# First offset convolution ahead of the second pair's sums, a new order of small sums and roundings, and the first result stored by halves

## The reference

```python
# block 1: a bottleneck with a modulated deformable 3x3 convolution
out = relu(group_norm(conv1x1(x, w1), gn1))            # 256 -> 64 channels, 32 groups
om = conv3x3(out, w_off) + b_off                       # 27 rows: 9 x offsets, 9 y offsets, 9 masks
sampled = bilinear_sample(out, py, px) * sigmoid(mask) # 9 taps
out = relu(group_norm(einsum(sampled, w2), gn2))
x = relu(group_norm(conv1x1(out, w3), gn3) + x)        # 64 -> 256 channels

# block 2: the same shape, weights rounded to powers of two, activations to 16 bits
h = conv1x1(quant(x), w1q)
h = relu(bn1(depthwise3x3(quant(h), pegq) + peg_b))
h = relu(bn2(conv3x3(quant(h), w2q)))
x = relu(bn3(conv1x1(quant(h), w3q)) + x)
# quant(t): scale = max(|t|)/32767; round(t/scale)*scale, one scale for the whole tensor
```

## Time and profile before

| what | us |
|---|---|
| runs | 90.78, 89.81, 90.74 |
| median | 90.74 |
| the profiled execution | 90.92 |
| its span, first to last instruction | 89.1 |

### The profile page before, as it was taken

The page is one execution under the profiler, slowest core; times in us unless marked ns, Lnnn a source line. Parts: engine busy times, 40 slices in busy tenths (PEclk is TensorE's granted clock), DMA queues, the critical chain, the costliest instruction groups (busy, mean ns, idle before and its releaser), DMA issues.

```text
span 89.1 us, 2173 instructions
## 1 busy us (share of the span) xinstructions
PE 74.9 (84%) x893; PEld 51.4 (58%) x893; DVE 64.8 (73%) x174; ACT 49.6 (56%) x88; POOL 5.0 (6%) x10
## 2 busy tenths in 40 slices
PE   5986999996899898999999999899579877779600
PEld 1332666474698797889988896355223374555400
DVE  0224539999999789999896725899895784867850
ACT  4203165679974999996868003807562254632660
POOL 7601010000000000000003100000000000000000
PEclk9999999999999999999999999999999999999999
DMA  1999800000000000000000000000000000000076
GB/s 29 328 318 324 329 9 0 0 7 0 0 7 0 0 0 7 4 11 0 0 7 0 0 0 7 0 0 0 0 0 0 0 0 0 0 7 4 0 256 215
DMA packets 3274, 4.17 MB, mean 47 GB/s; under 512 B 256, under 2 KB 2688, under 8 KB 3264
## 3 DMA queue, kind: packets, MB, share of 16 engines
q1 hardware_dynamic: 2992, 3.76, 12.7%
q10 hardware_dynamic: 272, 0.26, 0.9%
HBM read 2.98 MB, written 1.05 MB: 45 GB/s over the span
## 4 chain that ended last, share of the span: by engine, by line
PE 43%; DVE 29%; ACT 12%; DMA 6%; issue 4%; SPq 2%; DVEq 0%; ACTq 0%
PE acc L488 15%; PE slot L475 9%; DVE g_rows L912 9%; DMA x_sb<-x 6%; PE acc L616 4%; DVE g_cols L1014 3%; ACT g_cols L813 3%; PE acc L595 3%; PE slot L403 3%; ACT g_cols L720 2%; PE slot L524 2%; DVE g_cols L1055 2%; ACT pad L777 2%; PE slot L556 2%; DVE unused L1031 2%
## 5 line engine op out<-in xcount | busy, mean ns | idle before, releaser
L912 DVE TENSOR_TENSOR g_rows<-hats 128x2304 f32<-128x2304 f32 (+1 forms) x12 | 20.6, 1752 | 0.1
L720 ACT ACTIVATE g_cols<-slot 128x768 f32<-128x768 f32 x24 | 17.8, 830 | 3.7 <-PE slot L475 3.7
L488 PE MATMUL acc<-g_cols,v_sb 128*64 128x128 f32 x288 | 17.7, 276 | 0.0
L488 PEld LDWEIGHTS acc<-g_cols,v_sb 128*64 128x64 f32 x288 | 15.5, 137 | 1.1 <-issue 0.3
L366 PE MATMUL slot<-zeros 128*128 128x512 bf16 x54 | 14.8, 409 | 1.0 <-DVE zeros L832 1.0
L475 PE MATMUL slot<-consts_sb,g_rows 64*128 64x64 f32 x288 | 11.8, 226 | 2.1 <-DVE g_rows L912 1.7
L475 PEld LDWEIGHTS slot<-consts_sb,g_rows 64*128 64x128 f32 x288 | 10.3, 140 | 3.9 <-DVE g_rows L912 2.7
L366 PEld LDWEIGHTS slot<-zeros 128*128 128x128 bf16 x54 | 5.5, 109 | 6.9 <-issue 2.1
L777 ACT ACTIVATE pad<-g_cols 64x256 bf16<-64x256 int8 x8 | 3.3, 418 | 4.9 <-DVE g_cols L1055 4.8
L843 DVE BATCH_NORM_STATS2 stats<-acc 128x6 f32<-128x256 f32 x4 | 1.7, 431 | 4.3 <-PE acc L378 2.6
L403 PE MATMUL slot<-feat,woff_sb 128*64 128x256 f32 x36 | 4.7, 385 | 0.0
(11 more groups left out here) (137 smaller groups left out, 116.4 us busy)
## 6 DMA issues: line engine op xcount, KB each, us to landing
out<-g_cols SPq DMA_DIRECT2D x4, 256.0 KB, 2.3
x_sb<-x SPq DMA_DIRECT2D x3, 256.0 KB, 4.7
wq_sb<-wq SPq DMA_DIRECT2D x1, 484.5 KB, 6.5
woff_sb<-woff SPq DMA_DIRECT2D x1, 288.0 KB, 5.7
w_sb<-w SPq DMA_DIRECT2D x1, 288.0 KB, 5.8
x_sb<-x ACTq DMA_DIRECT2D x1, 256.0 KB, 3.1
w_sb<-w SPq DMA_DIRECT2D x1, 256.0 KB, 6.5
consts_sb<-consts SPq DMA_DIRECT2D x1, 232.0 KB, 5.7
```

The costliest lines, as they stand in the source:

```text
L488: mm = nc.tensor.matmul(acc[b2][rows(h), at:at + P], v_sb[:, B2 * h + b2, q, k, :], g_cols[t][h][:, NQ * k + q, :], start=(k == 0 and q == ...
L720: nc.scalar.activation(dst.rearrange("p k (r n) -> p k r n", r=HALVES), src.rearrange("p r (k n) -> p k r n", k=per), ACT.Copy).then_inc(g ...
L912: tt(g_rows[i % 3][:, taps], hats[:, t, h, 1, taps].unsqueeze(3).to_broadcast(shape), hats[:, t, h, 0, taps].unsqueeze(2).to_broadcast(sha ...
```

## The change

It has four parts.

1. PE's opening. The three idle matmuls before `pair_sums(2, 1)` go. Steps 0 and 1 of the offset convolution of pair 0 are issued ahead of `pair_sums(2, 1)`, steps 2 to 4 behind it; then comes `make_v(0)`, and only then the offset convolution of pair 1.
2. In the group norm over eight, for pair 1, the means matmul goes from ahead of the deviations matmul to behind `eight_vars`, with a semaphore `mean_done` of its own, which DVE now waits for.
3. The first rounding of block 2. DVE makes the quotients of (b2, c) = (0,0), (0,1 in image pair 1: written `quot[:, 0, 1]`) and `quot[:, 1, 1]`, and takes `ROUND` from `quot[:, 0, 0]` and `quot[:, 1, 1]`. ACT makes the quotient of `quot[:, 1, 0]` itself, and takes `ROUND` from it and from `quot[:, 0, 1]`. The indices of `quot` are c, then b2.
4. The first of four result pieces is handled and stored in two halves, one image each, so `PIECES` has five entries.

```diff
-PIECES = ((0, 0, 0, 2), (1, 0, 0, 2), (0, 1, 0, 2), (1, 1, 0, 2))
+PIECES = ((0, 0, 0, 1), (0, 0, 1, 1), (1, 0, 0, 2), (0, 1, 0, 2), (1, 1, 0, 2))
...
             conv1(1)
-            idle(IDLE[2], spare)
-            pair_sums(2, 1)
...
-            pe.wait_ge(woff_in, 16)
-            for b2 in range(B2):
-                pe.wait_ge(feat_ready, b2 + 1)
-                for s in range(TAPS_A):
-                    mm = om_step(b2, s)
-                    if b2 == 1 and s == 1:
-                        pe.wait_ge(consts_in, 16)
-                        om_turn(0)
-                mm.then_inc(om_done, 1)
...
-            for i in range(4):
+            pe.wait_ge(woff_in, 16)
+            pe.wait_ge(feat_ready, 1)
+            for s in range(TAPS_A):
+                mm = om_step(0, s)
+                if s == 1:
+                    pair_sums(2, 1)
+            mm.then_inc(om_done, 1)
+            pe.wait_ge(w2_in, 16)
+            make_v(0)
+            pe.wait_ge(feat_ready, 2)
+            for s in range(TAPS_A):
+                mm = om_step(1, s)
+                if s == 1:
+                    pe.wait_ge(consts_in, 16)
+                    om_turn(0)
+            mm.then_inc(om_done, 1)
+            for i in range(1, 4):
                 make_v(i)
...
-                nc.tensor.matmul(small[b2][:, 8:12], avg8, mv[:, b2, :, 0], start=True, stop=True)
+                if b2 == 0:
+                    nc.tensor.matmul(small[b2][:, 8:12], avg8, mv[:, b2, :, 0], start=True, stop=True)
...
+                if b2 == 1:
+                    nc.tensor.matmul(small[b2][:, 8:12], avg8, mv[:, b2, :, 0], start=True, stop=True
+                                     ).then_inc(mean_done, 1)
...
-                    if (b2, c) == LAST_WHOLE:
-                        pe.wait_ge(whole_by_dve, 1)
+                    if b2 == c:
+                        pe.wait_ge(whole_by_dve, b2 + 1)
                     else:
-                        pe.wait_ge(whole_by_act, CH * b2 + c + 1)
+                        pe.wait_ge(whole_by_act, b2 + 1)
...
+            a.wait_ge(inv_ready, 1)
+            by_act = flat(quot[:, 1, 0])
+            nc.scalar.activation(by_act, flat(y0[:, 1, 0]), ACT.Identity, bias=plus_round[:, 0:1],
+                                 scale=q_inv[:, 1:2]).then_inc(quot_by_act, 1)
+            a.wait_ge(quot_by_act, 1)
+            whole(by_act)
+            a.wait_ge(quot_ready, 2)
+            whole(flat(quot[:, 0, 1]))
...
-                    dve.wait_ge(sq_ready, b2 + 1)
+                    dve.wait_ge(mean_done, 1)
...
+            dve.wait_ge(relu_ready, 1)
+            quotient(1, flat(quot[:, 0, 0]), flat(y0[:, 0, 0]))
+            whole(flat(quot[:, 0, 0]), 1)
+            dve.wait_ge(relu_ready, 2)
+            quotient(1, flat(quot[:, 0, 1]), flat(y0[:, 0, 1]))
+            quotient(1, flat(quot[:, 1, 1]), flat(y0[:, 1, 1]))
+            whole(flat(quot[:, 1, 1]), 3)
...
-                dve.wait_ge(qconv_done, 3 * B2 + i + 1)
-                stt(res[:, c, b2], last_out(c, b2), bn_mul[:, 2 + c:3 + c],
-                    y0[:, c, b2], ALU.mult, ALU.add).then_inc(sum_ready, 1)
+                dve.wait_ge(qconv_done, 3 * B2 + CH * b2 + c + 1)
+                stt(res[:, c, b2, h:h + n], last_out(c, b2)[:, h:h + n], bn_mul[:, 2 + c:3 + c],
+                    y0[:, c, b2, h:h + n], ALU.mult, ALU.add).then_inc(sum_ready, 1)
```

More of the change, by code:

```diff
@@ L84 @@
 ROUND = 1.5 * 2.0 ** 23
-LAST_WHOLE = (1, 1)
+QUOTS = 3
 SQRT2 = 1.4142135623730951
@@ L183, in build @@
         minus_round = sb("minus_round", [P, 1])
+        plus_round = sb("plus_round", [P, 1])
         eps_sb = sb("eps_sb", [P, 1])
@@ L231, in build @@
         sq_done = sem("sq_done")
+        mean_done = sem("mean_done")
         var_ready = sem("var_ready")
@@ L264, in build @@
         quot_ready = sem("quot_ready")
+        quot_by_act = sem("quot_by_act")
+        inv_ready = sem("inv_ready")
         whole_by_act = sem("whole_by_act")
@@ L416, in om_turn @@
                 mm.then_inc(omt_done, 1)
-            pe.wait_ge(woff_in, 16)
-            for b2 in range(B2):
-                pe.wait_ge(feat_ready, b2 + 1)
-                for s in range(TAPS_A):
-                    mm = om_step(b2, s)
-                    if b2 == 1 and s == 1:
-                        pe.wait_ge(consts_in, 16)
-                        om_turn(0)
-                mm.then_inc(om_done, 1)
             v_banks = [small[0], small[1], acc[0], acc[1]]
-            pe.wait_ge(w2_in, 16)
             def make_v(i):
@@ L560, in spread_bias @@
             def spread_bias(n):
-                pe.wait_ge(quot_ready, CH * B2 + B2 * (n - 3) + 1)
+                pe.wait_ge(quot_ready, QUOTS + B2 * (n - 3) + 1)
                 nc.tensor.matmul(spread_of(n, 0), bn_off[:, n - 3:n - 2].to_broadcast([P, P]), ident,
@@ L629, in _ @@
                 if b2 == 0:
-                    pe.wait_ge(whole_by_dve, 2)
+                    pe.wait_ge(whole_by_dve, 3)
                 else:
-                    pe.wait_ge(whole_by_act, CH * B2)
+                    pe.wait_ge(whole_by_act, 3)
                 for c in range(CH):
@@ L780, in byte, with whole @@
                 return t.bitcast(dt).rearrange("p (n e) -> p n e", e=4)[:, :, n]
[L782 to L787, removed]
+            def whole(t):
+                nc.scalar.activation(t, t, ACT.Identity, bias=minus_round[:, 0:1]).then_inc(whole_by_act, 1)
+            a.wait_ge(inv_ready, 1)
[6 more added lines that the diff above has]
+            whole(flat(quot[:, 0, 1]))
             q2 = quot[:, 0, 0].rearrange("p b n -> p (b n)")
@@ L794, in high_parts @@
                         src = byte(q2[rows(h), N * b2:N * b2 + N], 1, I8)
-                        high_part(dst(b2, h), image(src), CH * B2 + B2 * (n - 2) + b2 + 1)
+                        high_part(dst(b2, h), image(src), QUOTS + B2 * (n - 2) + b2 + 1)
             a.wait_ge(pads_zero, 3)
@@ L804, in _ @@
                                          ).then_inc(act_ready, 1)
-            a.wait_ge(quot_ready, CH * B2 + 3 * B2)
+            a.wait_ge(quot_ready, QUOTS + 3 * B2)
             nc.scalar.activation(q2[:, N:2 * N], q2[:, N:2 * N], ACT.Identity, bias=minus_round[:, 0:1]
@@ L837, in _ @@
             nc.vector.memset(minus_round[:], -ROUND)
+            nc.vector.memset(plus_round[:], ROUND)
             dve.wait_ge(first_in, 16)
@@ L1034, in make_scale @@
                                                       q_scale[:, n:n + 1]))
-                settle(nc.vector.reciprocal(q_inv[:, n:n + 1], q_scale[:, n:n + 1]))
+                last = nc.vector.reciprocal(q_inv[:, n:n + 1], q_scale[:, n:n + 1])
+                if n == 1:
+                    last.then_inc(inv_ready, 1)
+                    dve.wait_ge(inv_ready, 1)
+                else:
+                    settle(last)
             eight_moments(0)
@@ L1063, in low_part, with whole @@
                 nc.vector.tensor_copy(dst, src).then_inc(lo_ready, 1)
[L1066 to L1073, removed]
+            def whole(t, done):
+                dve.wait_ge(quot_ready, done)
+                ts(t, t, ROUND, None, ALU.subtract).then_inc(whole_by_dve, 1)
+            dve.wait_ge(relu_ready, 1)
[5 more added lines that the diff above has]
+            whole(flat(quot[:, 1, 1]), 3)
             q2 = quot[:, 0, 0].rearrange("p b n -> p (b n)")
@@ L1092, in low_parts @@
                         low = byte(q2[rows(h), N * b2:N * b2 + N], 0, U8)
-                        low_part(dst(b2, h), image(low), CH * B2 + B2 * (n - 2) + b2 + 1)
+                        low_part(dst(b2, h), image(low), QUOTS + B2 * (n - 2) + b2 + 1)
                 quotients(0)
                 if n == 4:
-                    dve.wait_ge(quot_ready, CH * B2 + 2 * B2 + 1)
+                    dve.wait_ge(quot_ready, QUOTS + 2 * B2 + 1)
                     ts(q2[:, 0:N], q2[:, 0:N], ROUND, None, ALU.subtract).then_inc(whole_by_dve, 1)
```

## The result

The changed kernel took 91.86 us (median of 4 runs, 91.75 to 93.07), the kernel before 90.76 in the same comparison: a ratio of 1.0187 with a 95% interval of 1.0127 to 1.0246. It is slower, and by more than the forecast of 91.1. Repeated on the chip of the experiments it gave 91.97 against 90.70, 1.0183 (1.0130 to 1.0235). The profiled execution took 91.75, with a span of 90.0. Three of the changed kernel's ten runs took 93.07 to 93.24 us at a granted clock of 0.977 over the run; the ratios count two of them but not the run of 92.42 of the kernel before, and without the two they are 1.015 and 1.016 (those of the medians are 1.012 and 1.014).

The account below looks back on a forecast made before the run. No engine bounds it alone; up to about 31.5 us PE's make_v matmuls, ACT's copies and hats set the time. Parts 0.7 + 0 - 0.3 + 0 = +0.4 us on the 90.74 median gave 91.1, range 89.8 to 91.9.

Parts of the forecast that it names:

- Part 1, the length of the opening: PE's opening: make_v(0) alone takes 0.96 us plus 0.1 for a shape change; the three left still need two slots.
- Part 1, its beginning: PE's opening: offset weights land at 8.83, so the first offset steps start at 8.87; with the lone make_v, +0.7 us.
- The slower rival: PE's opening: offset weights land only at 9.30, delaying the second pair's sums; +1.0 us, 91.75; chance 0.21.
- The faster rival: PE's opening: the gap is really filled, each make_v costing 0.48 us anywhere; -0.95 us in all, 89.8; chance 0.18.
- Where ACT and DVE stood: Up to about 31.5 us: PE's make_v matmuls, ACT's copies and the hats set the time; DVE has 0.88 us to spare.
- Part 2: Group norm of pair 1, deviations ahead of means: DVE had not waited for ACT's root; price 0, bounds -0.1 and +0.2.
- Part 3: First rounding of block 2, shared by DVE and ACT: PE's start for pair 1 comes earlier, -0.3 us, bounds 0 and -0.4.
- The rival in which the rounding brings nothing: First rounding: ACT's quotient reads scale and bias from memory, so part 3 gives zero; sum +0.7, 91.4; chance 0.09.
- Part 4: Ending, first result in halves: data flow earlier, then pause, as the DMA rate sets the end; price 0, bounds -0.3 and +0.13.

## Why the prediction was wrong

It named the right mechanism and the right sign, and mis-sized one term: the credit for the earlier beginning of the opening. The forecast was +0.4 us on the median and "within 1%" as the likeliest; measured were 1.1 to 1.3 us, with 91.86 still inside the stated range.

- *Part 1, the length of the opening: right.* The prediction had the first step at 8.87 and ACT's copy 0.69 after 19.33, so 11.15 us between. Measured: 11.19 in four profiles. The lone `make_v` was put at 1.06 us and took 1.05; that the three that stay give nothing back is shown by one more in the gap costing nothing and a lone one in the old kernel lengthening the opening by 1.19.
- *Part 1, its beginning: the step that failed.* "Steps 0 and 1 of pair 0 start at 8.87, where `pair_sums(2, 1)` used to start at 9.49." The credit in this was 10.02-8.87 = 1.15 us. Both ends were off. The kernel before was profiled in an execution that began late (10.02; five other profiles with its opening lie at 9.35 to 9.87), and the changed one is held by the first pair's features and the offset weights until 8.95 to 9.53. The prediction let only the weights (8.83) hold PE there; it counted no wait for the features, which had ended at 8.54 in its one profile, where the first convolution took 1.30 us. In the changed openings they end at 8.81 to 9.39. The means are 9.78 and 9.20: a credit of 0.58. In the sum, 11.19-9.31-0.58 = +1.3 in place of +0.7. With the credits of 0.34 and 0.8 it would be +1.5 and +1.1.
- *The slower rival* was the late weights. In the chains of the six profiles with a changed opening the features came last in four and the weights in two, landing at 9.18 (the changed kernel's repeat, where the features end at 9.10) and 9.13, short of the rival's 9.30. The place was right (the wait ahead of PE's first step), the cause only in part; that its 91.75 lies 0.1 us from the measured time is in part luck.
- *The faster rival* needed a `make_v` that costs 0.48 us wherever it stands. It does not.
- *Where ACT and DVE stood:* the prediction took PE and ACT for what sets the time until about 31.5 and gave DVE 0.88 us to spare. At the third turn that holds after the change (23.18); before, DVE's `g_rows` ended within 0.04 us of them at 22.1, so earlier copies alone would not have started the third turn sooner.
- *Part 2: right*, no gain; the two runs with and without it agree (90.37 and 90.42 us).
- *Part 3: right*, -0.3 forecast, -0.29 in the trace, ratios of 0.9953 to 0.9977 in four runs that hold it with the old opening. ACT's quotient took 0.81 us and not the 0.72 of the sum, but PE's first load waits for DVE's part. The rival in which the rounding brings nothing falls.
- *Part 4: right*, nothing; the trace shows the pause that the prediction worked out. On the changed kernel's page a half of 128 KB takes 1.8 us from issue to landing and a whole of 256 KB 2.3.
- *The sum now:* +1.3-0.3+0 = +1.0, of the 1.10 and 1.27 between the medians. The rest, 0.1 to 0.3 us, is no more than the beginnings wander by, but no run shows that it lies there.

The version that beats both is the kernel before with the shared rounding, with or without part 2: 90.37 and 90.42 us, 0.3 to 0.4% less than before, and 1.6 to 1.7% less than the changed kernel.

## What to carry to other kernels

Where two small matmuls run side by side on TensorE, as `make_v`'s even and odd ones do here, the pair is the unit of work: moving one of them out of two pairs cost a whole slot in the gap and freed none where it came from (+1.19 us), and moving two cost no more than one. Move both or none. Before a wait is filled, look at what the filling stands in front of in the same queue: here the second pair's sums and all that follows from them. Look also at what the moved work itself waits for, since a wait that was hidden behind another comes forward with it. And take the beginning of a kernel from several executions, since a credit worked out against a single profile is only as good as that execution's first 10 us.

## What the runs showed of the hardware

The first microseconds of PE differ from run to run with the same code. The same first convolution of eight records took 1.30 us in the kernel before and 1.76 in the changed one, though nothing ahead of it had been changed on PE; over the eleven profiles with seven idle matmuls ahead of it, it took 1.28 to 1.98 us. The granted clock of that stretch is given as 1.00 in all of them, so it does not explain the difference, and the cause stays open:

```profile
3.98 1.30 PE L378 MATMUL acc<-x_sb,first_sb 128*64 128x256 f32 x8
```

```profile
4.08 1.76 PE L382 MATMUL acc<-x_sb,first_sb 128*64 128x256 f32 x8
```

An ACT piece of 512 columns that reads its scale and its bias from memory took 0.81 us, where the removals with a bias alone took 0.71 on average (0.70 to 0.72 in the kernel before): 0.10 more, once. And DVE and ACT could share one rounding without slowing DVE: its quotient took 0.49 us beside ACT's, 0.48 before.
